# A fused transformer-style block on one core: wider halves for the seven-product scheme, and condition terms fetched one step at a time

## The reference

```python
x = x + ffn0(cond0(x))            # agg_w[b] @ x[b] + agg_b ; (. @ B) @ A.T + bias
y = conv1d(x, weight, groups=4) + (c @ c_weight.T)[:, :, None] + fside[None, :, None]
logits = y @ gate_w.T + expert_bias; e = argmax(logits)     # 4 experts
x = x + y @ W_up.T + lora_B[e] @ (lora_A[e] @ y)            # rank 8
```

## Time and profile before

| | us |
|---|---|
| median of 3 executions | 1102.08 (1099.69 to 1104.13) |
| time of the profiled execution | 1100.2 |
| span of the profiled execution (first to last instruction) | 1098.4 |
| TensorE busy (matmul) | 1074.8 |
| VectorE busy | 906.2 |
| ScalarE busy | 601.1 |

### The profile page before, as it was taken

One profiled execution on the slowest core, in us unless ns is written; L12 is line 12 of the kernel. 1 busy time (PEld: TensorE's weight loads), 2 busy tenths in 40 slices (PEclk: granted clock), 3 DMA queues, 4 the chain that ended last, 5 costly groups with the idle time before them and its releaser, 6 DMA issues.

```text
span 1098.4 us, 19163 instructions
## 1 busy us (share of the span) xinstructions
PE 1074.8 (98%) x7034; PEld 1046.9 (95%) x7034; DVE 906.2 (83%) x1665; ACT 601.1 (55%) x1231; POOL 7.9 (1%) x22
## 2 busy tenths in 40 slices
PE   5799999999999999999999999999999999999998
PEld 5699999999999999999999999999999999999998
DVE  7998888888888888888888888888888887888774
ACT  6675556555556555556555555555555565555441
POOL 2000000000000000000000000000000000000000
PEclk9999999999999999999999999999999999999999
DMA  9945544455544455544455544455444455543422
GB/s 332 292 125 139 153 132 117 111 143 155 148 135 115 114 145 154 147 136 113 113 149 154 142 139 110 116 148 155 138 139 109 120 148 157 138 136 89 98 59 78
DMA packets 118732, 152.19 MB, mean 139 GB/s; under 512 B 21904, under 2 KB 92304, under 8 KB 118512
## 3 DMA queue, kind: packets, MB, share of 16 engines
q1 hardware_dynamic: 116752, 148.71, 49.3%
q10 hardware_dynamic: 1888, 2.27, 0.6%
HBM read 81.03 MB, written 35.95 MB: 106 GB/s over the span
## 4 chain that ended last, share of the span: by engine, by line
PE 91%; DVE 5%; issue 1%; DMA 1%; SPq 0%; ACT 0%; DVEq 0%
PE M L1506 41%; PE H L1506 9%; PE G L1506 9%; PE F L1455 8%; PE F L1405 7%; PE F L1375 3%; PE F L1376 3%; PE F L1377 3%; PE M L1429 2%; PE G L1429 2%; PE M L1541 2%; DMA Lr<-in_Ld_dram 1%; DVE Wsl L1124 1%; PE F L1393 1%; PE F L1392 1%
## 5 line engine op out<-in xcount | busy, mean ns | idle before, releaser
L1506 PE MATMUL M<-Wsh,yh 128*128 128x384 f32 x896 | 308.3, 344 | 0.0
L1506 PE MATMUL M<-Wsl,yh 128*128 128x384 f32 x896 | 302.7, 338 | 0.0
L1506 PE MATMUL M<-Wsh,yl 128*128 128x384 f32 x896 | 302.1, 337 | 0.0
L976 DVE STREAM_TRANSPOSE yr<-F 128x512 f32<-128x512 f32 x126 | 90.1, 716 | 110.5 <-PE F L1455 110.4
L1506 PEld LDWEIGHTS M<-Wsh,yh 128*128 128x128 f32 x896 | 168.4, 188 | 3.6 <-DVE yl L1027 0.3
L1506 PEld LDWEIGHTS M<-Wsl,yh 128*128 128x128 f32 x896 | 168.7, 188 | 2.7
L1506 PEld LDWEIGHTS M<-Wsh,yl 128*128 128x128 f32 x896 | 168.2, 188 | 0.0
L486 ACT ACTIVATE yh<-yr 128x1024 fp32r<-128x1024 f32 (+1 forms) x127 | 120.2, 948 | 20.5 <-DVE yr L991 15.5
L598 ACT ACTIVATE F<-G,cbX 128x128 f32<-128x128 f32 x248 | 69.0, 341 | 79.9 <-PE G L1429 79.9
L598 ACT ACTIVATE F<-M,cbX 128x128 f32<-128x128 f32 x248 | 69.0, 341 | 63.8 <-PE M L1429 63.8
L486 ACT ACTIVATE F<-biasb 128x512 f32<-128x512 f32 x124 | 74.4, 601 | 43.3 <-DVE yr L976 40.8
(11 more groups left out here) (219 smaller groups left out, 2526.8 us busy)
## 6 DMA issues: line engine op xcount, KB each, us to landing
x<-in_xP_dram SPq DMA_DIRECT2D x64, 516.0 KB, 4.3
xTr<-in_xT_dram SPq DMA_DIRECT2D x64, 512.0 KB, 3.8
Xr<-x SPq DMA_DIRECT2D x502, 64.5 KB, 2.5
out_dram<-x SPq DMA_DIRECT2D x62, 516.0 KB, 3.0
agb<-agb_scratch SPq DMA_DIRECT2D x31, 128.0 KB, 3.5
agg<-agg_scratch SPq DMA_DIRECT2D x60, 32.0 KB, 3.3
Wsr<-in_Wsd_dram ACTq DMA_DIRECT2D x2, 768.0 KB, 8.5
Wsr<-in_Wsd_dram SPq DMA_DIRECT2D x2, 768.0 KB, 6.0
```

The source lines that it names most:

```text
L976: dve.transpose(dst.rearrange("p j k m -> p (j k) m").rearrange("p (k r) (g b n) -> p g b k r n", r=2, g=2, b=4)[:, g % 2], F[g % 2][:, :] ...
L1506: last = pe.matmul(dst, w[:, y, k, :], m, start=fresh and n_ == 0, stop=k == 3 and n_ == 2, skip_group_check=True)
```

## The change

Two numbers and the layout of columns change. HW goes from 384 to 412 columns, and the full products keep 200 columns of W_up, so that CW = 4 + 32 + 200 = 236. The three column parts are now cut by the 25 leading places (CN) of each of the eight groups of 128 instead of by whole groups. To make room on chip for the wider weights, `cbX` is laid over a part of the buffer `yl` that step 0 uses late, is written to DRAM once (`cb_out`), and 16 values of each partition, those of one step, are loaded before each step into `cbs` (`load_cb`). `pc` waits for that load, and `S4(0)`, which is the first to write over `cbX`, waits until it has been written out and read. `lora` gets two waits that later entries of the queue had. Nine small vectors get one common buffer (`few`). The last stores are cut 4 and 4 groups instead of 5 and 3.

```diff
-CW = 292
-HW = 384
+CN = 25
+CW = E + E * R + 8 * CN
+HW = 4 * (128 - CN)
...
+    cbD = nc.dram_tensor("cb_scratch", (128, NS, 4 * NG), fp32, kind="Internal").ap()
...
-        cbX = sb("cbX", [128, NG, NB])
...
+        cbs = sb("cbs", [128, 4 * NG])
...
+        cbX = over("cbX", "yl", [128, NS, NG, 4], 3072)
...
             if c == 1:
-                return o.rearrange("p r a -> p (r a)")[:, 388:644]
-            return o[:, 0:3, 1:129] if c == 0 else o[:, 5:8, 0:128]
+                return bass.AP(o.tensor, o.offset + 1, [o.ap[0], (4 * 129 - 1, 2), (129, 4), (1, CN)])
+            return o[:, 0:4, 1 + CN:129] if c == 0 else o[:, 4:8, CN:128]
...
+            def cb_out():
+                sp.wait_ge(v_cb, 4)
+                sp.dma_start(cbD, cbX.rearrange("p s g b -> p s (g b)")).then_inc(d_cbw, 16)
+
+            def load_cb(s):
+                if s >= NS:
+                    return
+                if s == 1:
+                    sp.wait_ge(d_cbw, 16)
+                else:
+                    sp.wait_ge(a_pc, 4 * s)
+                sp.dma_start(cbs[:, :], cbD[:, s, :]).then_inc(d_cb, 16)
...
             def lora():
                 sp.wait_ge(p_agb, 2)
+                sp.wait_ge(d_gw, 16)
+                sp.wait_ge(d_gg, 128)
                 sp.dma_start(Lr[:, :], Ld).then_inc(d_l, 16)
...
             lora()
+            cb_out()
             load_x2(3)
             rx(1, 0)
+            load_cb(1)
             load_agb(2)
...
                 store(2 * it - 2)
+                load_cb(it + 1)
                 load_x(2 * it + 4)
...
-            last_store(NT - 2, 0, 5, 2)
-            last_store(NT - 1, 3, 8, 4)
-            last_store(NT - 1, 0, 3, 5)
-            last_store(NT - 2, 5, 8, 6)
+            last_store(NT - 2, 0, 4, 2)
+            last_store(NT - 1, 4, 8, 4)
+            last_store(NT - 1, 0, 4, 5)
+            last_store(NT - 2, 4, 8, 6)
...
                 act.wait_ge(p_p, 4 * (s - 1) + g + 1)
+                if g == 0:
+                    act.wait_ge(d_cb, 16 * s)
...
-                                          ACT.Identity, bias=cbX[:, g, 4 * s + b:4 * s + b + 1])
+                                          ACT.Identity, bias=cbs[:, 4 * g + b:4 * g + b + 1])
...
             def S4(s):
                 dve.wait_ge(v_s, 4 * s + 3)
-                if s > 0:
+                if s == 0:
+                    dve.wait_ge(d_cbw, 16)
+                    dve.wait_ge(a_pc, 4)
+                else:
                     dve.wait_ge(p_m, NBK * (s - 1) + 11)
...
                 dst = x1_part(2 * s, 1)
-                dve.tensor_tensor(dst, G[:, 36:CW], dst, ALU.add).then_inc(v_f, 1)
+                dve.tensor_tensor(dst, G[:, 36:CW].rearrange("p (h c a) -> p h c a", h=2, c=4), dst, ALU.add).then_inc(v_f, 1)
...
-                lo, hi = ((0, 384), (384, 640), (640, 1024))[c]
+                lo, hi = ((0, HW), (HW, L - HW), (L - HW, L))[c]
```

More of the change, by code:

```diff
@@ L109, in adaln_ffn @@
         yr = over("yr", "yl", [128, 7, 4, 128])
[L110 to L113, removed]
         zm = sb("zm", [128, E * R])
+        few = sb("few", [128, 25])
+        csB, fsB, ebb, wts = few[:, 0:1], few[:, 1:5], few[:, 5:9], few[:, 9:13]
+        lg, mx, sc, m2 = few[:, 13:17], few[:, 17:18], few[:, 18:22], few[:, 22:23]
+        warmd = few[:, 23:25]
         zs = sb("zs", [128, 96])
@@ L171, in adaln_ffn @@
         g_con, g_wk, g_cc = (sem(n) for n in ("g_con", "g_wk", "g_cc"))
-        d_mlp, d_b, d_a, d_bi, d_cc, d_fs, d_t, d_l, d_eb = (
-            sem(n) for n in ("d_mlp", "d_b", "d_a", "d_bi", "d_cc", "d_fs", "d_t", "d_l", "d_eb"))
+        d_cbw, d_cb, d_mlp, d_b, d_a, d_bi, d_cc, d_fs, d_t, d_l, d_eb = (
+            sem(n) for n in ("d_cbw", "d_cb", "d_mlp", "d_b", "d_a", "d_bi", "d_cc", "d_fs", "d_t", "d_l", "d_eb"))
         d_wk = [sem(f"d_wk{h}") for h in range(2)]
@@ L561, in cbp @@
                 copy(F[g % 2][:, :].rearrange("p (b n) -> p b n", b=4),
-                     cbX[:, g, 0:4].unsqueeze(2).broadcast_to([128, 4, 128])).then_inc(a_pc, 1)
+                     cbX[:, 0, g, :].unsqueeze(2).broadcast_to([128, 4, 128])).then_inc(a_pc, 1)
             def xs(s, q):
@@ L1041, in addU @@
                 dst = x1_part(2 * s + 1, 0)
-                dve.tensor_tensor(dst, bankB(s)[:, 0:HW].rearrange("p (c a) -> p c a", c=3), dst, ALU.add).then_inc(v_ux, 1)
+                dve.tensor_tensor(dst, bankB(s)[:, 0:HW].rearrange("p (c a) -> p c a", c=4), dst, ALU.add).then_inc(v_ux, 1)
             def addV(s):
@@ L1075, in f11 @@
                 dst = x1_part(2 * s, 0)
-                dve.tensor_tensor(dst, bankA(s)[:, 0:HW].rearrange("p (c a) -> p c a", c=3), dst, ALU.add).then_inc(v_f, 1)
+                dve.tensor_tensor(dst, bankA(s)[:, 0:HW].rearrange("p (c a) -> p c a", c=4), dst, ALU.add).then_inc(v_f, 1)
             def fG(s):
@@ L1091, in fH @@
                 dst = x1_part(2 * s + 1, 1)
-                dve.tensor_tensor(dst, H[:, 36:CW], dst, ALU.add).then_inc(v_f, 1)
+                dve.tensor_tensor(dst, H[:, 36:CW].rearrange("p (h c a) -> p h c a", h=2, c=4), dst, ALU.add).then_inc(v_f, 1)
             def f21(s):
@@ L1096, in f21 @@
                 dst = x1_part(2 * s + 1, 0)
-                dve.tensor_tensor(dst, M[2][:, 0:HW].rearrange("p (c a) -> p c a", c=3), dst, ALU.add).then_inc(v_f, 1)
+                dve.tensor_tensor(dst, M[2][:, 0:HW].rearrange("p (c a) -> p c a", c=4), dst, ALU.add).then_inc(v_f, 1)
             def f12(s):
@@ L1101, in f12 @@
                 dst = x1_part(2 * s, 2)
-                dve.tensor_tensor(dst, bankB(s)[:, 0:HW].rearrange("p (c a) -> p c a", c=3), dst, ALU.add).then_inc(v_f, 1)
+                dve.tensor_tensor(dst, bankB(s)[:, 0:HW].rearrange("p (c a) -> p c a", c=4), dst, ALU.add).then_inc(v_f, 1)
             def evac(c):
@@ L1172, in cb @@
                 dve.wait_ge(p_cb, 1)
-                dve.tensor_scalar(cbX[:, g, :], G[:, 128 * g:128 * g + 128], fsB[:, g:g + 1], None, ALU.add).then_inc(v_cb, 1)
+                dve.tensor_scalar(cbX[:, :, g, :], G[:, 128 * g:128 * g + 128].rearrange("p (s b) -> p s b", b=4), fsB[:, g:g + 1], None, ALU.add).then_inc(v_cb, 1)
             def t1():
```

14 lines of the change are left out of this document (5 added, 9 removed).

## The result

Medians: 1099.41 us after (22 executions, 1098.48 to 1100.86), 1101.70 us before (22 executions, 1099.69 to 1104.13). The ratio is 0.998, with a 95% interval of 0.9974 to 0.9986: the change takes away 2.3 us. The forecast was no difference, 1102.1 us. The profiled execution took 1098.67 us, with a span of 1096.9.

The account below looks back on a forecast made before the run. TensorE's dense matmul stream was taken to bound the kernel. Steps -0.9, start +0.9 and end 0 us sum to 0 on the profiled 1100.2; with the median 1.9 above, 1102.1 us, range 1098.5 to 1107.

Parts of the forecast that it names:

- What bounds the kernel: In 31 of 32 steps TensorE alone bounds: 220 matmuls as a stream, 33.00 us a step, priced by distance between starts.
- The floor at 236 columns: Kind c products in each step: a floor of about 111 ns per 128 x 128 stationary block makes 236 columns cost 111.5 ns.
- no floor: Rival, chance 0.12: 236-column products follow the line to 109.7 ns, so the steps give -3.8 us.
- a higher floor: Rival, chance 0.10: the 48 kind c products cost more than 111 ns; at 119 ns the kernel takes 1114 us.
- the fallback to fp32's cost: Rival, chance 0.02: fp32r products under 256 columns cost four times the columns, 421 ns, +440 us, 1542 in all.
- `unit_dl` of the middle part 0.11: Sign of being right: in a step's chain, the middle part's `unit_dl`, two 200-column products at 111.5 ns each, takes 0.11 us.
- the price of a matmul by width: Step's matmuls priced by columns, about 0.446 ns each above the floor: 412 columns +12.5 ns, 236 columns -23.2; -0.029 us a step.
- What lies beside it in a step: VectorE's changed rows, 25-element runs and `load_cb` within a step were claimed to cost nothing.
- a new wait in every step: Rival, chance 0.04: `cbs` lands after `pc` needs it, or 25-element runs take over 5 us; 0.3 us a step gives 1112.
- The start and end: Start: wider VectorE rows and SP's new entries cost +0.9 us, bounds 0 and +1.8; end: larger last store, 0.
- the first of the two cases named: SP's queue at the start: `load_agb(2)` and `load_xT(3, 0)` come 1.1 us later by issue time alone.
- the line with a free start: Fast end of the range: 236 columns at the line's 109.7 ns and a start costing nothing, put at 1098.5 us.

Follow-up runs that it names:

- a_c128: The changed kernel with its 48 full products (kind c) a step cut from 236 to their first 128 columns; 1099.23 us.
- b_pad32: The kernel before with 32 free bytes ahead of the activation buffers; 1102.14 us.
- b_moved64: b_moved with its activation buffers 64 bytes higher; 1100.87 us, ratio 0.9995.
- b_yh416: The kernel before with 416 free bytes ahead of `yh`, so only `yh`, `yl` and the small buffers behind them move; 1098.79 us.
- b_moved: The kernel before with `cbX` and five small buffers placed last and 64 free bytes in their place, so activation buffers lie as in a_cn32; 1096.78 us, ratio 0.9961.
- a_cn32_pad: a_cn32 with 2688 free bytes behind the weights, putting every later buffer where the changed kernel has it; 1102.54 us, ratio 1.0009.
- a_cn32: The changed kernel with the old widths (CN = 32, 384 and 292 columns), everything else of the change kept; 1095.97 us, ratio 0.995.
- b_again: The kernel before, unchanged, executed once more with a profile; 1101.04 us.

## Why the prediction was wrong, point by point

**What bounds the kernel**: right. The chain of a step is TensorE alone, dense, and the whole change is in the distances between starts.

**The floor at 236 columns**: right for the products of kind c. Predicted 111.5 ns, measured 111.8; 128 columns give nothing more (a_c128). Its rivals fall: no floor (109.7 ns), a higher floor (from 113.5 on) and the fallback to fp32's cost. 48 products of kind c gave -1.097 us a step where -1.114 stood. The price of 236 columns hardly moved with the addresses (111.82 and 111.92), and neither did that of 408 (188.10 to 188.14). But the floor does not stand "under every matmul": the two 200-column products of `unit_dl` take 93.6 ns where 111.5 stood, and the sign "`unit_dl` of the middle part 0.11" did not come. Its four wide products cost more than forecast, so that `unit_dl` came to +0.034 us against +0.035; that these agree is luck.

**The failed step** is "the price of a matmul by width" and the sum made of it. I took the price of a matmul as a matter of its width alone, and left the 72 wide matmuls that the change does not touch at nothing. They gave 0.070 us. Kind s gave another 0.045, as 412 columns cost 11.96 ns more than 384 and not 12.5, and kind c 0.017 less than forecast: that is the way from -0.029 to -0.130. In place of this the runs showed that the price also depends on where the buffers lie: with every instruction the same, a step takes 33.03, 33.01, 33.00, 32.94 or 32.84 us (b_pad32, before, b_moved64, b_yh416, b_moved). That spread of 0.19 us is larger than the forecast of -0.029 and the measured -0.130. The step's length was therefore not to be had from widths alone: the same widening brings -0.126 us at one set of places and +0.134 at another, 3.8 us less or 4.0 more over 30 steps. At the first, kind s costs 11.35 ns more and kind c 22.96 less; at the second, kind s 13.11 more, kind c 21.94 less, and 256 columns go from 117.86 to 118.90. The forecast, 12.5 and 23.2, lies between for kind s.

The pair at fixed places (a_cn32_pad and after) also shows a size that was wrong. There the unchanged 72 matmuls do not get cheaper (+0.004 us), and nearly the whole gap to the forecast is kind s: 11.35 ns for 28 columns are 0.405 a column, and the prediction took 0.446, 84 x 1.15 = 0.097 us. That slope had been drawn from 292 columns of kind c to 384 of kind s, as if both kinds lay on one line.

So the net 2.3 us are not the worth of the seven-product scheme on more columns. How the changed kernel's -0.130 is shared between widths and addresses depends on the corner from which one starts: before and a_cn32_pad have nearly the same length (33.011 and 33.007), so on the path before, a_cn32_pad, after the places bring -0.004 and the widths -0.126. The -0.004 are a balance: the unchanged 72 matmuls get 0.074 us cheaper and kind s 0.051 dearer.

**What lies beside it in a step**: right. No wait for `cbs` at `pc`, no head-of-step idle on TensorE, 25-element runs free; the rival of a new wait in every step falls.

**The start and end**: the size was somewhat low, +0.9 predicted within bounds of 0 and 1.8. Median minus 30 steps gives 110.9 to 111.5 for the three kernels with the old code (before, b_moved, b_moved64), 111.9 and 112.3 for the new code with old widths (a_cn32, a_cn32_pad), 112.3 to 113.0 for the wider ones. The means are 111.3, 112.1 and 112.7, which makes about +0.8 for the condition terms' path and +0.6 for wider weights, 1.4 in all. Inside each of the three groups the values differ by 0.4 to 0.7, so this split is rough. By its steps: VectorE's wider rows take 1.87 and 1.13 us (1.87 and 1.14 by the prediction's 1.03 ns an element). SP's two new entries put `xTr` off by the issue time alone, the first of the two cases named. ScalarE's wait grew from 0.78 to 1.14 us. One profile can't size this, for the start of an unchanged kernel moves by 0.95 us (b_again). A part of it is TensorE's clock. The changed kernel's records (timeline, start and length):

```profile
47.89 0.41 PE L1464 MATMUL F<-Xh,Th 128*128 128x256 f32 x1
48.10 0.42 PE L1464 MATMUL F<-Xh,Tl 128*128 128x256 f32 x1
...
49.94 0.28 PE L1397 MATMUL F<-xTl,Bh 128*128 128x256 f32 x1
50.06 0.28 PE L1398 MATMUL F<-xTh,Bl 128*128 128x256 f32 x1
```

256 columns stand 0.21 us apart, then 0.12: up to 49.8 us this is the lower of the two levels, 1.2 GHz, at a granted clock of 0.57 over 46 to 50 us. TensorE was busy 4.83 of the 8 us from 42 to 50. In a_c128 it was busy 4.72 of the same 8, and the clock stayed at 1.00; in before it stayed at 1.00 too, and in b_again, the same program, it was 0.50 from 38 to 42 us. It comes and goes between executions in this part, and the time of the unchanged kernel follows it. In the executions of before that stood beside the experiments the mean time is 1100.6 us where the granted clock of the whole execution is 0.998 (18 of them), 1101.5 at 0.997 (28) and 1102.7 at 0.994 (9). That is a spread as large as the change's 2.3 us, so only medians of many executions can show a difference of this size. The 22 executions of the changed kernel show no such order. The prediction's "clock at full level in all 40 slices" was read too strongly: a 9 is nine tenths or more, and before stood at 0.57 from 26 to 30 us.

**The sum**: -3.9 + 1.4 = -2.5 against -2.3 measured. The 1099.41 us lie inside the stated range and within 0.5% of no difference, but the change is clear of its own interval, where none was forecast, and neither its size nor its sign could be had from the widths as they were priced. The range's ends don't follow from their terms: the line with a free start gives 1098.3 and not 1098.5, a floor of 113.5 ns with 1.8 us of start gives 1106.2 and not 1107. The fastest version is a_cn32, the changed kernel with the old widths, at 0.995.

**What stays open**: why a matmul's distance depends on addresses. Shown are the effect itself, that moving `yh` and `yl` changes kind s, and that 384 columns follow `yh` modulo 512 in the eight executions looked at while 408 and 412 do not. Not explained are the 0.039 us between b_moved and a_cn32 and the cheaper 512 columns of b_yh416. An obvious rival is that other engines' accesses to the moved buffers get in TensorE's way. The traces speak against it: inside the runs of kind s, 384 columns stand 176.0 ns apart while VectorE idles and 175.7 to 176.5 while it works (before), 174.5 against 174.6 to 175.1 in b_moved. As the same product meets the same work in every step, this is a hint and no proof. It was not tried to move the weights alone, or to sweep one buffer through 512 bytes.

## What to carry to other kernels

Where TensorE is dense, a change of some columns must be weighed against what a move of buffers alone does, here up to 0.2 us in 33 (0.6% of a step): measure the old widths at the new addresses as well before the gain is credited to the widths. In this kernel, products that bring a 128-column stationary block each gained next to nothing under about 244 fp32r columns in a run. When a kernel is otherwise finished, try its buffers in other places; 64 bytes were worth 4 us here.

## What the runs showed of the hardware that was not expected

- The same 220 matmuls in the same order take 32.84 to 33.03 us a step by the places of the on-chip buffers (b_moved, b_pad32), and repeated to 0.002 us in the two executions with the same places (before, b_again).
- The place of the two buffers with the stationary operands counts (b_yh416, twelve products of 384 columns in 2.10 us instead of 2.11, kind s 177.02 instead of 177.67 ns). The Trainium skill, "TensorE: Matmul & The Clock Gate", section "Step-by-step: what each phase is for", says that loading the next weights does not steal read bandwidth from the running matmul; these runs show no lost bandwidth as such, but a price that changed when only `yh`, `yl` and the small buffers behind them were moved.
- The floor of 111 ns binds only in a run: the lone 200-column products of `unit_dl`, which stand between longer ones, take 93.6 ns (after), and the first 128-column product of a run takes 0.06 us. What is gained there is paid behind: the first 412-column product after such a run takes 0.24 us (a_c128, 126.27 to 126.51) where the next ones take 0.19.
